# Local attention: the mask of out-of-reach keys moved from TensorE products to GpSimd selections, with a new loop order

## The reference

```python
sim = jnp.einsum('bhwid,bhwjd->bhwij', bq, bk)     # bk: the block before, and the block itself
mask = (i < j) | (i > j + WINDOW) | (j == -1)
sim = jnp.where(mask, -jnp.finfo(sim.dtype).max, sim)
attn = jax.nn.softmax(sim, axis=-1)
out = jnp.einsum('bhwij,bhwjd->bhwid', attn, bv)
```

## Time and profile before

| | |
|---|---|
| median of 3 runs | 1795.65 us (1794.73 to 1807.06) |
| the profiled execution's own time | 1800.07 us |
| its span, first to last instruction | 1798.5 us |
| TensorE busy | 1713.6 us (95%), weight loads 1304.6 |
| VectorE, ScalarE, GpSimd busy | 1146.4 (64%), 999.9 (56%), 862.7 (48%) |
| mean granted TensorE clock | 0.958 |
| mask products of local attention (L1218) | 1024, mean about 220 ns each |

### The profile page before, as it was taken

The page is one execution under the profiler, slowest core; times in us unless marked ns, Lnnn a source line. Parts: engine busy times, 40 slices in busy tenths (PEclk is TensorE's granted clock), DMA queues, the critical chain, the costliest instruction groups (busy, mean ns, idle before and its releaser), DMA issues. The chain is left out here.

```text
span 1798.5 us, 42022 instructions
## 1 busy us (share of the span) xinstructions
PE 1713.6 (95%) x13984; PEld 1304.6 (73%) x13984; DVE 1146.4 (64%) x2853; ACT 999.9 (56%) x1927; POOL 862.7 (48%) x886
## 2 busy tenths in 40 slices
PE   5999999999889999999989999899999999899997
PEld 3656656666567777777768888677777777678886
DVE  6567667777886676676643344776766776445554
ACT  2566566665745565555555455465555565555443
POOL 3333343333644665644643333565545665345453
PEclk7799899989999999999999999899999999999999
DMA  6544554434111011110023212101111010212221
GB/s 178 175 121 119 159 158 146 132 109 146 49 60 36 1 34 35 35 35 24 15 81 105 70 61 81 48 13 35 35 35 35 0 35 23 84 61 91 93 82 47
DMA packets 102327, 129.64 MB, mean 72 GB/s; under 512 B 15834, under 2 KB 70788, under 8 KB 102276
## 3 DMA queue, kind: packets, MB, share of 16 engines
q1 hardware_dynamic: 96084, 106.44, 20.2%
q0 software_dynamic: 6192, 22.55, 3.6%
HBM read 82.55 MB, written 46.15 MB: 72 GB/s over the span
## 5 line engine op out<-in xcount | busy, mean ns | idle before, releaser
L454 ACT ACTIVATE a_PT<-b 128x384 f32<-128x384 f32 (+1 forms) x384 | 183.5, 523 | 132.7 <-PE b L676 77.3
L491 DVE TENSOR_REDUCE a_negm<-d 128x2 f32<-128x256 f32 (+3 forms) x256 | 201.7, 813 | 63.3 <-PE d L637 60.7
L907 POOL TENSOR_TENSOR l_t<-l_t,l_t 128x512 f32<-128x512 f32 x128 | 165.3, 1297 | 113.8 <-DVE l_t L1059 113.6
L1077 DVE CUSTOM_DVE_ANT_0 d<-d,window 128x256 f32<-128x256 f32 (+1 forms) x512 | 184.0, 420 | 22.8 <-PE d L1176 22.5
L991 ACT ACTIVATE l_PT<-b 128x512 f32<-128x512 f32 (+1 forms) x256 | 125.4, 542 | 100.9 <-PE b L1218 98.9
L1476 POOL TENSOR_TENSOR m_hid_lo<-m_hid,m_hid_hi 128x512 fp32r<-128x512 f32 x80 | 103.4, 1302 | 160.9 <-ACT m_hid_hi L1537 160.8
L921 POOL TENSOR_TENSOR l_PS<-l_PT 128x768 f32<-128x768 f32 x64 | 117.6, 1838 | 117.5 <-ACT l_PT L991 117.5
L1104 PE MATMUL d<-w,l_xt 128*128 128x512 f32 x384 | 164.6, 429 | 2.2 <-DVE l_t L1059 2.2
L379 POOL TENSOR_SCALAR_AFFINE_SELECT a_PT<-a_PT 128x512 f32<-128x512 f32 x128 | 79.8, 648 | 157.9 <-ACT a_PT L454 157.9
L1105 PE MATMUL d<-w,l_xt 128*128 128x512 f32 x384 | 152.0, 396 | 0.0
L1106 PE MATMUL d<-w,l_xt 128*128 128x512 f32 x384 | 151.6, 395 | 0.0
(11 more groups left out here) (222 smaller groups left out, 4866.4 us busy)
## 6 DMA issues: line engine op xcount, KB each, us to landing
qk_parts<-a_qk_hi SPq DMA_DIRECT2D x64, 256.0 KB, 2.7
a_Q<-qk_parts SPq DMA_DIRECT2D x64, 192.0 KB, 3.5
a_K<-qk_parts SPq DMA_DIRECT2D x64, 192.0 KB, 4.4
qk_parts<-a_qk_lo SPq DMA_DIRECT2D x32, 256.0 KB, 3.1
xin<-after_attn SPq DMA_DIRECT2D x32, 256.0 KB, 3.1
m_xr<-after_attn SPq DMA_DIRECT2D x16, 512.0 KB, 4.0
after_attn<-rows_out POOLq DMA_DIRECT2D x14, 512.0 KB, 5.3
xin<-in_L_attn_x SPq DMA_DIRECT2D x8, 512.0 KB, 3.4
```

Of the source, the lines that this page charges most:

```text
L454: nc.scalar.activation(PT[:, p // PG % 2, 2 * (p % PG) + hh, QOFF[t]:QOFF[t] + nq], SC[hh][:, 0:nq], ACT.Exp, scale=AD ** -0.5).then_inc(e ...
L491: dve.tensor_reduce(negm[:, q, 2 * p:2 * p + 2], MX[i % 2][:, :, 0:nk], AX.X, ALU.max, negate=True).then_inc(max_done, 1)
L907: pool.tensor_tensor(t1[:, par, w, :], t1[:, par, w, :], t2[:, par, w, :], ALU.add)\
L1077: m = dve.tensor_tensor_reduce(out=o, in0=o, in1=mask, scale=-1.0, scalar=-NEG, op0=ALU.add, op1=ALU.min, accum_out=negm[:, q + t, p // 2, ...
```

## The change

Only the mask on the same block (`blk` 0) stays a product: 4 per unit instead of 8. The mask on the next block's queries is put on behind the exponentials: a new step `ms:i` of GpSimd runs two selections (`affine_select`, one per head) of 128x384 elements of `PT`, which set the entries out of reach to zero and signal `masked`. `ps` and `pv` wait for `masked` instead of `exp_done`. `STEPS` and two of the joins have a new order; in the joins only GpSimd's entries `ms` and `ps` are placed anew.

```diff
     STEPS = parse("""
-        f_x:0 f_xe:0 sm:4 st:0 f_qk:0 f_qe:0 f_qe:1 f_qk:1 st:1 sm:5 ps:0 f_qk:2 f_iv:0 f_qe:2 ps:1 st:2
-        f_qe:3 f_qk:3 st:3 sm:6 f_iv:1 f_qe:4 f_qk:4 f_qk:5 sm:7 f_qe:5 z:0 f_iv:2 zn:0 pv:0 sv:0 f_qk:6
-        f_qe:6 mt:1 f_qe:7 f_qk:7 st:4 f_iv:3 pv:1 st:5 ps:2 z:1 sv:1 st:6 f_t:0 zn:1 pv:2 f_te:0 z:2 sv:2
-        f_sm:0 f_te:1 f_t:1 zn:2 ps:3 st:7 f_sm:1 f_t:2 zs:0 pv:3 f_te:2 f_sm:2 zs:1 zs:2 f_te:3 f_t:3 sv:3
-        f_sm:3 z:3 xr:0 f_v:0 zn:3 zs:3 f_v:1 f_mt:0 f_v:2 out:0 out:1 out:2 f_v:3 out:3""")
+        f_x:0 f_xe:0 st:0 ms:0 sm:4 f_qk:0 f_qe:0 st:1 sm:5 ps:0 f_qe:1 f_qk:1 st:2 f_qk:2 f_iv:0 ms:1 sm:6
+        f_qe:2 st:3 f_qk:3 f_qe:3 f_iv:1 ps:1 z:0 sm:7 zn:0 f_qe:4 pv:0 sv:0 f_qk:4 mt:1 f_qe:5 f_qk:5 st:4
+        f_iv:2 f_qk:6 f_qe:6 ms:2 f_qe:7 st:5 f_qk:7 pv:1 f_iv:3 z:1 sv:1 zn:1 zs:0 st:6 ps:2 pv:2 f_te:0
+        f_t:0 st:7 f_te:1 f_t:1 z:2 zn:2 sv:2 ms:3 f_t:2 ps:3 zs:1 f_sm:0 pv:3 f_te:2 xr:0 f_sm:1 zs:2 f_t:3
+        f_te:3 z:3 sv:3 f_sm:2 zn:3 f_v:0 f_v:1 f_sm:3 zs:3 f_v:2 f_v:3 f_mt:0 out:0 out:1 out:2 out:3""")
@@ gpsimd
+            elif name == "ms":
+                wait_apart(pool, K, exp_done, 2 * (b * UNITS + 2 * i + 2))
+                for hh in range(2):
+                    past = PT[:, i % 2, hh, 0:TB - 1, P:2 * P]
+                    pool.affine_select(out=past, in_=past, compare_op=ALU.is_ge, fill=0.0, base=0,
+                                       pattern=[[0, TB - 1], [-1, P]], channel_multiplier=1).then_inc(masked, 1)
             elif name == "ps":
-                pool.wait_ge(exp_done, 2 * (b * UNITS + 2 * i + 2))
+                pool.wait_ge(masked, 2 * (b * PAIRS + i + 1))
@@ tensor
                 for n, table in enumerate((K["window"], K["window_sw"])):
-                    for blk in range(2):
-                        for hh in range(2):
+                    for hh in range(2):
+                        m = pe.matmul(SC[hh][:, :].rearrange("p (t b q) -> p t b q", t=2, b=2)
+                                      [:, :, 0, at:at + FD], table[rows, 1, :],
             elif name == "pv":
-                pe.wait_ge(exp_done, 2 * (b * UNITS + 2 * i + 2))
+                pe.wait_ge(masked, 2 * (b * PAIRS + i + 1))
@@ JOINS, second and fourth
-        sm:4 ps:0 nz:0 nx:0 st:0 xr:0 sm:5 +f_n:0 st:1 ps:1 sm:6 st:2 sm:7 ns:0 pv:0 z:0 sv:0 st:3 nw:0 zn:0
+        sm:4 nz:0 nx:0 st:0 xr:0 sm:5 +f_n:0 st:1 ms:0 ps:0 sm:6 st:2 sm:7 ns:0 pv:0 z:0 sv:0 st:3 ms:1 ps:1 nw:0 zn:0
```

More of the change, by code:

```diff
@@ L828, in local_attention @@
     mx_full, max_done, sc_full, exp_done = sem("mx_full"), sem("max_done"), sem("sc_full"), sem("exp_done")
-    ps_done = sem("ps_done")
+    ps_done, masked = sem("ps_done"), sem("masked")
     mt_full, mrow_done = sem("mt_full"), sem("mrow_done")
@@ L1214, in do @@
                 for n, table in enumerate((K["window"], K["window_sw"])):
-                    for blk in range(2):
-                        for hh in range(2):
[L1217 to L1224, removed]
+                    for hh in range(2):
+                        rows, at = slice(FD * hh, FD * hh + FD), FD * (hh ^ n)
+                        m = pe.matmul(SC[hh][:, :].rearrange("p (t b q) -> p t b q", t=2, b=2)
+                                      [:, :, 0, at:at + FD], table[rows, 1, :],
+                                      K["identb"][rows, FD * hh:FD * hh + FD].unsqueeze(1)
+                                      .to_broadcast([FD, 2, FD]), start=False, stop=True,
+                                      skip_group_check=True)
+                        if n == 1:
+                            m.then_inc(sc_full, 1)
             elif name == "pv":
-                pe.wait_ge(exp_done, 2 * (b * UNITS + 2 * i + 2))
+                pe.wait_ge(masked, 2 * (b * PAIRS + i + 1))
                 pe.wait_ge(z_done, b * PAIRS + i)
@@ L1722 @@
     parse("""
-        sm:4 ps:0 nz:0 nx:0 st:0 xr:0 sm:5 +f_n:0 st:1 ps:1 sm:6 st:2 sm:7 ns:0 pv:0 z:0 sv:0 st:3 nw:0 zn:0
-        mt:1 st:4 pv:1 zs:0 ns:1 st:5 nm:0 z:1 sv:1 ps:2 +f_m:0 ps:3 st:6 zs:1 zn:1 pv:2 z:2 sv:2 zn:2 st:7
+        sm:4 nz:0 nx:0 st:0 xr:0 sm:5 +f_n:0 st:1 ms:0 ps:0 sm:6 st:2 sm:7 ns:0 pv:0 z:0 sv:0 st:3 ms:1 ps:1 nw:0 zn:0
+        mt:1 st:4 pv:1 zs:0 ns:1 st:5 ms:2 nm:0 z:1 sv:1 ps:2 +f_m:0 st:6 zs:1 zn:1 pv:2 z:2 sv:2 zn:2 st:7 ms:3 ps:3
         +f_t:0 zs:2 +f_te:0 pv:3 z:3 zs:3 sv:3 zn:3 +f_w1:0 +set:0 out:0 out:1 out:2 out:3 ns:2 +f_h:0
@@ L1733 @@
     parse("""
-        nx:0 sm:4 st:0 +f_n:0 st:1 sm:5 nz:0 ns:0 ps:0 pv:0 sm:6 st:2 sv:0 sm:7 z:0 ps:1 st:3 ps:2 mt:1 zs:0
-        +f_m:0 ps:3 pv:1 st:4 nm:0 st:5 zn:0 z:1 sv:1 st:6 pv:2 zn:1 zs:1 ns:1 sv:2 z:2 st:7 zn:2 +f_t:0 nw:0
+        nx:0 sm:4 st:0 +f_n:0 st:1 ms:0 sm:5 nz:0 ns:0 ps:0 pv:0 sm:6 st:2 sv:0 sm:7 z:0 st:3 ms:1 ps:1 mt:1 zs:0
+        +f_m:0 pv:1 st:4 nm:0 st:5 ms:2 ps:2 zn:0 z:1 sv:1 st:6 pv:2 zn:1 zs:1 ns:1 sv:2 z:2 st:7 ms:3 ps:3 zn:2 +f_t:0 nw:0
         zs:2 +f_te:0 pv:3 sv:3 xr:0 z:3 zs:3 zn:3 +f_w1:0 out:0 out:1 out:2 out:3 +set:0 ns:2 +banks:0 +f_h:0
```

## The result

The changed kernel takes 1827.33 us (median of 4, 1822.20 to 1831.52), the kernel before beside it 1796.10 us (median of 4, one of them 1807.06). The ratio taken over all these runs is 1.0153, with a 95% interval of 1.0123 to 1.0182, so the change is slower by about 1.5%, 27 us; the two medians alone give 31 us, 1.0174. The profiled execution's span is 1824.9 us where the earlier trace rows and the rest of the front come from one of 1798.5.

What follows compares the result with a forecast made beforehand. TensorE, 100% busy in the loops, was taken as the bound: -0.88 + 0.65 + 0.9 + 0.7 + 0.2 = +1.57 us a round, x14 = +22, joins +2, so 1795.65 + 24 is 1819 us; range 1797 to 1832.

Steps and rivals of the forecast that it cites:

- Products removed: TensorE, loop rounds: the mask products left out save 0.11 us a unit, 8 units, so -0.88 us a round.
- `f_qk:0`: Loop round: this projection can't start sooner after the transpositions than now, +0.1 us a round.
- Switches: TensorE, loop rounds: four more changes of tile class, some 0.2 us each, taken as +0.65 us a round; bounds 0 and 0.8.
- class C: Tile class of the `pv` and `sv` products, 64 columns; changes to or from it counted among those of some 0.2 us.
- pv:2: Loop round: TensorE waits here for `zn:1`, whose chain begins at `sv:1`'s end; +0.9 us a round.
- f_t:2 and pv:3: Loop round: `f_t:2` 0.4 us late for VectorE's reads, `pv:3` 0.3 for `zn:2`; together +0.7, bounds 0.3 and 1.0.
- The 0.1 at `f_v:0`: Loop round: VectorE's queue after `zn:2` ends about 0.1 us after `f_v:0` wants its bank.
- GpSimd: Loop round: selections of 0.5 us; `f_t:0`'s operands ready at 31.3 us, `f_t:0` at 31.7, so nothing added.
- Joins: Two joins: `ms:3` puts 1.05 us in each, the second also at `pv:1`; less removed products, +2 us in all.
- (a): Rival: TensorE stays without gaps, the waits met by misjudged slack; -4 us, 1791 us; chance 0.12.
- (b): Rival: only `pv:2` waits, `f_t:2` and `pv:3` don't; +0.75 us a round, 1808 us; chance 0.18.
- (c): Rival: GpSimd becomes the bound, strided selections taking 0.92 us each; 29 us on top, 1848 us; chance 0.10.

Runs made afterwards that it cites:

- two_switches: Kernel before with one unit of scores (`st:1`) moved between the first two pieces of the queries' and keys' projection; round 54.57 us against 53.85.
- loops_alone: Changed kernel, but both joins with the tables and mask products of before; 1820.03 us (ratio 1.0101), round 55.40 us.
- sums_first: Changed kernel with `sv:1` put ahead of `pv:1` and a semaphore of its own for the sums; round 55.29 us, span 1819.6 us.
- no_select: Changed kernel without the selections on GpSimd, that mask left out; 1813.47 us (ratio 1.0079), round 55.40 us.

## Why the prediction was right or wrong, point by point

- **The verdict** (slower by over 1%) and its mechanism held: 14 loop rounds of +1.57 us were forecast, +1.55 measured, 22.0 us both.
- **Products removed**, -0.88: the 0.11 us a unit is right, in both orders. That it is gained in every unit is not: taking them out alone gives 0.70 in the new order. The part lost at `f_qk:0` was in the sum (+0.1), and so was that lost in `pv:2`'s wait, by the 1.28 us of `st:6`; so the sum holds, though the bare product term overstates what the idea brings.
- **Switches**, +0.65 for four: 0.18 us each by two_switches, 0.7, if those with class C cost the same. The trace's rows gave the size; "in size too" says more of the page than it states.
- **pv:2**, +0.9: measured 0.92 (`st:6` and the wait are 2.20 us together). Right in size, but not the sole cause. The prediction did say that `f_t:0` would wait without it; the price, 0.5, was too low (0.9), since I took GpSimd's end for that of a full queue. It is a chain from `f_qk:7`, and it ends nearly as late without the selections.
- **f_t:2 and pv:3**, +0.7: 0.36 (`sv:2` and `f_t:2` take 2.41 us where 2.05 was reckoned) and 0.38. Right. The 0.1 at `f_v:0` did not come.
- **GpSimd**: selections of 0.525 us for 0.5 forecast, the last scaling at 31.5 us into the round for 31.3, `f_t:0` at 31.8 for 31.7.
- **Joins**, +2: measured -3.1. The term was about right for the code at full clock and wrong for the profile that it was set against. At like clock the joins of before's tables take 40.1 and 40.5 us (loops_alone), that of the change 42.0 (second join of sums_first), and 42.0 less the 4 x 0.37 = 1.5 us of its dip in the first: about +2. But before's own joins are 8.1 us longer than those of loops_alone, some 7 of it by the clock (0.92 in both), and the change's lost some 3.4 (0.96 in both). I took no account of either.
- **The start**, +7.6, was not forecast, and no line of the change lies in it.
- **The total**: 1819 us forecast, 1827 measured, in the range. That +24 lies so near the 26.4 of the two spans is in part luck: the loops gave the +22.0 forecast, but the joins gave -3.1 for +2, and the start +7.6 for nothing. The medians differ by 31 us. Some 4 of the 7 missing are the step that I took from the profiled execution of before, 1800.07 us, down to its median, while the changed kernel's profiled execution, 1826.42, lies beside its own. What those 4 us were is not shown, as before has one trace. An estimate from the table: its joins were 8.1 us longer than those of loops_alone, its start 5.4 earlier than the average of the other 13 kernels, which leaves 2.7.
- Of the rivals, (a) and (b) fell with both waits there, (c) with no_select.

## What to carry to other kernels

Where TensorE never waits, a new order has no idle time to win and can bring waits: price it before the saving that it is to make possible, by laying TensorE's steps end to end against each dependent chain (here `f_qk:7` to `f_t:0` and `sv:1` to `pv:2`). One wait can stand in front of another of the same length; test them together. A part that costs the loop nothing (the selections) can still cost in the joins; take the whole kernel's time beside the round's. And read the granted clock of each stretch of the profile of before, since a dip in it is a time that a change may seem to gain or lose.

## What the hardware showed that I had not expected

- VectorE and GpSimd slow each other where VectorE adds two operands from SBUF: its sum (L1074) began while GpSimd's scalings (L919, to 714.87 + 2.04 = 716.91) still ran and took 1.09 us, where its product of the same size with one operand from PSUM (L1068) takes 0.68 (no run shows this sum with GpSimd idle); GpSimd's sum beside it took 1.72 us, where such sums average 1.293 in the changed kernel, and its selections averaged 601 ns for 525. The Trainium skill (SBUF — State Buffer, Who interferes with whom, and SBUF: two separate sides) tells of one port pair that the two engines must take in turn, for VectorE operations with two SBUF inputs too; these rows agree: L1074 overlaps the scalings ahead of it by 0.54 us and GpSimd's sum overlaps L1074 by 0.59, and each lost about 0.4 us.
- The join whose weights came 1.15 us later was some 4 us longer, 3.4 of it by the clock, which fell after TensorE's stops.
